# A two-product graph step with layer norm on one core: tiles in groups of four, sorted splits, two transpose banks

## The chip, the cores and the metric

The kernel runs on one core of a Trainium2 chip. Its time is the device time in microseconds, a median over runs. The matrix engine is called PE, its weight loads PEld, the vector engine DVE, the scalar engine ACT, GpSimd POOL, and SP is the engine that issues the transfers.

## What is computed

`adj` is 2048 x 2048 and `x` is 2048 x 512, both fp32:

```python
A_s  = (adj + adj.T) * 0.5 + eye(N)
deg  = sum(A_s, axis=1)
dinv = where(deg > 0, deg ** -0.5, 0)
y    = (adj @ (dinv[:, None] * A_s * dinv[None, :])) @ x
out  = layernorm(x + y, eps=1e-5)          # no scale, no shift
```

(In the reference `adj` is passed both as the matrix that is made symmetric and as the left factor.)

## The kernel before

The product is taken from the right. First u = dinv * (A_s @ (dinv * x)), which is the stage of the **steps**; then y = adj @ u, the stage of the **columns**. Both need fp32 precision from a reduced-precision product, so every operand is split into a high part (ACT rounds it) and a low part (DVE subtracts), and each product of a 128 x 128 tile with a 128 x 512 tile is three matmuls: high by high, high by low, low by high. There are 768 matmuls in the steps and 768 in the columns.

**A tile** is 128 rows of `adj`, there are 16. For each the kernel loads a strip (its rows, 128 x 2048) and needs the same columns turned. Tiles 0 to 3 are loaded as columns (`col`), turned by PE against the identity into a PSUM bank in four batches of four (`transpose_batch`), and copied to AT by ACT (`copy_turned`). Tiles 4 to 15 are loaded straight into AT (`load_pair`, two tiles in four transfers) in such a way that a 32 x 32 transpose on DVE (`turn`) finishes them. `sum_rows` adds the turned tile to the strip in place and sums the row, which is one DVE operation of 2048 elements; ACT takes the root of the degree, DVE inverts it, POOL refines it (DVE for tiles 0 to 3), and then `z_high` and `z_low` split dinv * x of the tile.

**A step** is one half (8 of the 16 row tiles) of one strip: `s_high` on ACT and `s_low` on DVE split 1024 columns of the strip into SH and SL, of which there are two pairs, and PE makes 24 matmuls over 8 banks (`step`). `SEGMENTS` lists the 32 steps: a segment keeps one half in the banks, and at its end the banks are saved (`save_part`, ACT) or added (`add_part`, DVE) to `part`. In the first segment only seven banks take part, since bank 7 is the one that the transposes of tiles 2 and 3 use; the eighth row tile's splits are kept in KH and KL and multiplied behind step 3 (`bank7_first_segment`). The second halves of tiles 8 to 11 are loaded and summed a second time (`load_again`, `sum_again`, `AGAIN`), because their strips are given away before.

**A pair of tiles** (4 and 5, 6 and 7, ...) interleaves its rows one by one: tile t has every second row. So the weights of a tile in a split half are every second column for tiles 4 to 15 and contiguous for 0 to 3 (`own_columns`, `half_weights`).

**The columns** are 32 halves of 24 matmuls, 16 column tiles by two halves (`HALVES`). `column_high` and `column_low` split 1024 elements of the turned matrix out of AT, one operation for the upper half and two of 512 for the lower. PE waits for `atl_done`. `layer_norm` follows each column tile.

**The order** on each engine is a list written out by hand in the code; every wait is on a semaphore of another engine. SP issues the transfers one after another and stands still at each of its waits: a strip waits until its place's last `s_low` is done, and an x tile for its buffer; the load of pair 8 waits for the end of step 3 and stands behind the strips and x tiles of tiles 4 to 7.

The lines in the profile that matter: L805 the transposes on PE, L817 to L861 the products of the steps, L897 to L899 the columns, L371 the copies of turned tiles, L389 and L391 `s_high`, L405 `z_high`, L432 `column_high`, L536 `turn`, L539 `sum_rows`, L588 `s_low`, L600 `z_low`, L620 `add_part`, L738 `column_low`.

## Time and profile before

| | us |
|---|---|
| median of 3 runs | 419.74 (418.32 to 422.92) |
| the profiled execution | 421.51 |
| its span, first to last instruction | 419.4 |
| PE busy in it | 381.2 (91%) |
| DVE busy | 244.6 (58%) |
| ACT busy | 118.4 (28%) |

The span is what the trace shows, and the profiled execution's time is 2.1 us more than it. The chain of waits is the work that ended last, followed back. Matmul starts are what to read of PE, since the ends are modelled and overlap the next matmul.

### The profile page before, as it was taken

The numbers are of one execution on the slowest core, as the hardware profiler recorded it, in microseconds if no ns is written. First come the engines' busy times: TensorE is split into PE (matmuls) and PEld (weight loads), VectorE is DVE, ScalarE is ACT, GpSimd is POOL, SyncE is SP. The second block draws the span as 40 slices with busy tenths as digits, with TensorE's granted clock in tenths as the row PEclk, the third lists the DMA queues.
The fourth block names the chain that finished last, engine by engine and source line by source line (L and its number), as shares of the span: only waits on it lengthen the run. The fifth ranks groups of instructions, "written<-read, shape, count | busy, mean of one in ns | idle before, by whom it ended". The sixth has DMA issues, their size and how long they took to land.

```text
span 419.4 us, 4227 instructions
## 1 busy us (share of the span) xinstructions
PE 381.2 (91%) x1600; PEld 308.8 (74%) x1600; DVE 244.6 (58%) x435; ACT 118.4 (28%) x186; POOL 23.6 (6%) x59
## 2 busy tenths in 40 slices
PE   3696699998999878998799999999999999999993
PEld 2575488776887756886588788888888888888882
DVE  1643638775739496679539952663444555555454
ACT  3443431315332112121326432222222112222210
POOL 0011101111031111002200000000000000000000
PEclk9998699999999988999899999999999999999999
DMA  7999139992799999430100000130111111111102
GB/s 233 337 346 186 52 107 245 315 184 72 213 218 279 272 243 308 152 100 25 52 26 0 2 0 2 50 101 2 50 50 52 50 50 52 50 51 51 34 31 86
DMA packets 68659, 49.54 MB, mean 118 GB/s; under 512 B 50848, under 2 KB 59040, under 8 KB 66720
## 3 DMA queue, kind: packets, MB, share of 16 engines
q1 hardware_dynamic: 68640, 49.29, 46.5%
q8 instruction: 12, 0.20, 0.2%
q14 instruction: 7, 0.06, 0.0%
HBM read 45.09 MB, written 4.19 MB: 118 GB/s over the span
## 4 chain that ended last, share of the span: by engine, by line
PE 64%; DVE 17%; DMA 6%; ACT 5%; issue 4%; SPq 3%; POOL 0%; ACTq 0%; DVEq 0%
PE bank L897 14%; PE bank L899 14%; PE bank L898 14%; PE bank L846 7%; PE bank L849 7%; PE bank L843 6%; DVE strip L539 5%; DVE SL L588 3%; DVE AT L536 3%; DMA col<-in_adj 2%; ACT SH L391 2%; DMA AT<-in_adj 2%; SPq L250 2%; DMA xr<-in_x 2%; PE bank L805 2%
## 5 line engine op out<-in xcount | busy, mean ns | idle before, releaser
L897 PE MATMUL bank<-UH,ATH 128*128 128x512 f32 x256 | 100.8, 394 | 0.4 <-DVE ATL L738 0.4
L899 PE MATMUL bank<-UH,ATL 128*128 128x512 f32 x256 | 100.7, 393 | 0.0
L898 PE MATMUL bank<-UL,ATH 128*128 128x512 f32 x256 | 100.5, 393 | 0.0
L738 DVE TENSOR_TENSOR ATL<-AT,ATH 128x512 fp32r<-128x512 f32 (+1 forms) x48 | 40.3, 867 | 77.2 <-ACT ATH L432 77.2
L432 ACT ACTIVATE ATH<-AT 128x512 fp32r<-128x512 f32 (+1 forms) x48 | 35.4, 768 | 84.1 <-PE bank L899 84.1
L897 PEld LDWEIGHTS bank<-UH,ATH 128*128 128x128 f32 x256 | 49.1, 192 | 11.0 <-DVE ATL L738 0.8
L588 DVE TENSOR_TENSOR SL<-strip,SH 128x1024 fp32r<-128x1024 f32 (+1 forms) x32 | 38.5, 1203 | 31.6 <-ACT SH L391 31.2
L849 PE MATMUL bank<-ZHr,SL 128*128 128x512 f32 x128 | 52.8, 413 | 4.4 <-DVE SL L588 4.4
L899 PEld LDWEIGHTS bank<-UH,ATL 128*128 128x128 f32 x256 | 49.1, 192 | 10.4
L898 PEld LDWEIGHTS bank<-UL,ATH 128*128 128x128 f32 x256 | 49.1, 192 | 10.2
L843 PE MATMUL bank<-ZHs,SH 128*128 128x512 f32 x117 | 48.2, 412 | 7.7 <-ACT ZHs L405 7.5
L846 PE MATMUL bank<-ZLr,SH 128*128 128x512 f32 x128 | 52.4, 410 | 2.8 <-DVE ZLr L600 2.8
L843 PE MATMUL bank<-ZHr,SH 128*128 128x512 f32 x128 | 52.4, 409 | 2.7 <-ACT SH L391 2.7
L539 DVE SCALAR_TENSOR_TENSOR strip<-strip,AT 128x2048 f32<-128x2048 f32 (+1 forms) x19 | 37.0, 1950 | 23.9 <-ACT AT L371 17.9
L846 PE MATMUL bank<-ZLs,SH 128*128 128x512 f32 x117 | 47.8, 409 | 3.3 <-DVE ZLs L600 3.3
L849 PE MATMUL bank<-ZHs,SL 128*128 128x512 f32 x117 | 47.1, 403 | 0.2 <-DVE SL L588 0.2
L391 ACT ACTIVATE SH<-strip 128x1024 fp32r<-128x1024 f32 x28 | 29.3, 1050 | 33.6 <-PE bank L849 33.5
L849 PEld LDWEIGHTS bank<-ZHr,SL 128*128 128x128 f32 x128 | 25.6, 200 | 11.4 <-DVE SL L588 6.1
L843 PEld LDWEIGHTS bank<-ZHs,SH 128*128 128x128 f32 x117 | 23.2, 198 | 13.3 <-ACT SH L389 8.1
L843 PEld LDWEIGHTS bank<-ZHr,SH 128*128 128x128 f32 x128 | 25.8, 202 | 9.3 <-ACT SH L391 4.0
L846 PEld LDWEIGHTS bank<-ZLr,SH 128*128 128x128 f32 x128 | 25.6, 200 | 9.0 <-DVE ZLr L600 3.5
L536 DVE STREAM_TRANSPOSE AT<-AT 128x2048 f32<-128x2048 f32 x12 | 27.6, 2303 | 5.6 <-DMA AT<-in_adj 5.6
(66 smaller groups left out, 281.4 us busy)
## 6 DMA issues: line engine op xcount, KB each, us to landing
strip<-in_adj SPq DMA_DIRECT2D x15, 1024.0 KB, 8.1
AT<-in_adj SPq DMA_DIRECT2D x24, 512.0 KB, 9.2
xr<-in_x SPq DMA_DIRECT2D x32, 256.0 KB, 2.9
out<-outr SPq DMA_DIRECT2D x16, 256.0 KB, 2.0
col<-in_adj SPq DMA_DIRECT2D x3, 1024.0 KB, 10.0
strip<-in_adj SPq DMA_DIRECT2D x4, 512.0 KB, 9.3
col<-in_adj SPq DMA_DIRECT2D x4, 256.0 KB, 5.0
strip<-in_adj SPq DMA_DIRECT2D x4, 256.0 KB, 5.3
```

The costliest lines, as they stand in the source:

```text
L391: nc.scalar.activation(SH[s % 2][:, :], s_half(s), ACT.Copy).then_inc(sh_done, 1)
L432: ins = nc.scalar.activation(half_place(ATH[i % 2], lo, hi, groups), src, ACT.Copy)
L536: nc.vector.transpose(v, v).then_inc(turned, 1)
L539: return nc.vector.scalar_tensor_tensor(out=strip[t % 4][:, cols], in0=strip[t % 4][:, cols], scalar=1.0, in1=turned_rows(t, cols.start, c ...
L588: nc.vector.tensor_tensor(SL[s % 2][:, lo:HALF], s_half(s)[:, lo:HALF], SH[s % 2][:, lo:HALF].bitcast(F32), ALU.subtract).then_inc(sl_done, 1)
L738: ins = nc.vector.tensor_tensor(half_place(ATL[i % 2], lo, hi, groups), src, half_place(ATH[i % 2], lo, hi, groups).bitcast(F32), ALU.subt ...
L843: nc.tensor.matmul(banks[b][:, :], wh, zh[:, :], start=first, stop=False)
L846: nc.tensor.matmul(banks[b][:, :], wh, zl[:, :], start=False, stop=False)
L849: nc.tensor.matmul(banks[b][:, :], wl, zh[:, :], start=False, stop=stop).then_inc(prod_done, 1)
L897: nc.tensor.matmul(bank[:, :], wh, UH[:, k, :], start=opens and n == 0, stop=False)
L898: nc.tensor.matmul(bank[:, :], wh, UL[:, k, :], start=False, stop=False)
L899: last = nc.tensor.matmul(bank[:, :], wl, UH[:, k, :], start=False, stop=ends)
```

## The change

- Tiles 4 to 15 come in **groups of four** (`GROUPS`): a tile has eight consecutive rows in every 32 (`R = 8`), instead of every second row. `load_block` loads four tiles by 2 parts of 1024 rows, in runs of 128 columns (512 bytes) instead of 64 (256 bytes); `turn` does half a tile (1024 elements) for each part, so there are 24 of them and not 12.
- The splits **sort** the columns (`sorted_pieces`): high and low are written so that each tile's 128 columns lie together. A step on half 0 takes two operations of 512 for it, one on half 1 one of 1024. The weights of all tiles are contiguous (`weights`, `half_weights`). In the columns both halves are split in two operations of 512.
- The **first segment** has four pairs SH and SL (`S_SLOT`), so that the splits of steps 0 to 3 all stay; steps 0 to 2 run on six banks (`early_step`), banks 6 and 7 take the transposes of tiles 1 to 3 in turn, and their share of steps 0 to 2 follows (`late_banks`) ahead of step 3. KH and KL are gone.
- The **second load** of the halves of tiles 8 to 11 is gone with its sums; `SEGMENTS` has another order of tiles, and the strips other places (`STRIP_SLOT`).
- x is loaded into the place of the low split (`XZ`), in seven places; an x tile waits for the products that used the place before, so on SP, where strips stand behind it.
- The **order lists** of ACT and DVE are new.

The core of the diff:

```diff
 Q = 32
+R = 8
...
-    PAIRS = range(NATURAL, NB, 2)
-    SEGMENTS = [(0, [0, 1, 2, 3]), (1, [0, 1, 2, 3, 4, 5, 6, 7]), (0, [4, 5, 6, 7, 8, 9, 10, 11, 12, 13]),
-                (1, [12, 13, 8, 9, 10, 11, 14, 15]), (0, [14, 15])]
+    EARLY = 3
+    LATE_BANKS = (6, 7)
+    GROUPS = range(NATURAL, NB, 4)
+    SEGMENTS = [(0, [0, 1, 2, 3]), (1, [0, 1, 2, 3, 4, 5, 6, 7]), (0, [4, 5, 6, 7, 8, 9, 10, 11]),
+                (1, [9, 10, 11, 8, 12, 13, 14, 15]), (0, [13, 14, 15, 12])]
     STEPS = [(t, half) for half, tiles in SEGMENTS for t in tiles]
     SEG_START = [sum(len(tiles) for _, tiles in SEGMENTS[:i]) for i in range(len(SEGMENTS) + 1)]
     S_END = len(STEPS)
...
+    STRIP_SLOT = [2, 3, 0, 1] * 3 + [3, 0, 1, 2]
+    S_SLOT = [s % 4 if s < HB else s % 2 for s in range(S_END)]
...
+            rows = ap[group_of(t) * P:(group_of(t) + 4) * P, :]
+            return rows.rearrange("(x k i) c -> k x i c", k=4, i=R)[t % 4]
...
+        def sorted_pieces(s, buf):
+
+            v = s_half(s)
+            if STEPS[s][1] == 0:
+                lo, hi = slice(0, HALF // 2), slice(HALF // 2, HALF)
+                return [(v[:, lo], buf[:, lo]),
+                        (v[:, hi].rearrange("p (x k i) -> p x k i", k=4, i=R),
+                         buf[:, hi].rearrange("p (k x i) -> p x k i", k=4, i=R))]
+            return [(v.rearrange("p (x k i) -> p x k i", k=4, i=R), buf.rearrange("p (k x i) -> p x k i", k=4, i=R))]
+
+        def weights(buf, half, b):
+
+            n = b if half == 0 else b % 4 * 2 + b // 4
+            return buf[:, n * P:(n + 1) * P]
...
+            def load_block(first, part):
+                rows = slice(part * HALF, (part + 1) * HALF)
+                for q in range(4):
+                    c0 = first * P + P * q
+                    dst = AT[Q * q:Q * (q + 1), first * N:(first + 4) * N].rearrange(
+                        "p (b e) -> p b e", e=P)[:, part * HALF // Q:(part + 1) * HALF // Q, :]
+                    src = adj[rows, c0:c0 + P].rearrange("(b r) c -> r b c", r=Q)
+                    sp.dma_start(dst, src).then_inc(block_in[first, part], 16)
 
...
+                t, slot = Z_TILES[k], z_slot(k)
+                if z_before(k) is not None:
+                    sp.wait_ge(prod_done, step_end(z_before(k)))
+                sp.dma_start(XZ[slot][:, :], own_rows(x, t)).then_inc(xz_in[slot], 16)
...
-            load_pair(4)
+            load_block(4, 0)
+            load_block(4, 1)
             load_strip(4)
             load_x(4)
             load_strip(5)
             load_x(5)
-            load_pair(6)
             load_strip(6)
             load_x(6)
             load_strip(7)
             load_x(7)
...
-            sp.wait_ge(prod_done, step_end(SEG_START[1]))
-            sp.wait_ge(zl_done, EARLY_X)
-            load_pair(8)
+            sp.wait_ge(tr_copied, CHUNKS * NATURAL)
+            load_block(8, 0)
+            load_block(8, 1)
+            load_x(8)
             load_strip(8)
-            load_x(8)
+            load_x(9)
             load_strip(9)
-            load_x(9)
-            load_pair(10)
+            load_x(10)
...
+            sp.wait_ge(prod_done, step_end(Z_LAST[7]))
+            load_block(12, 0)
             load_x(11)
+            load_block(12, 1)
+            load_x(12)
...
+                if s_before(s) is not None:
+                    act.wait_ge(prod_done, step_end(s_before(s)))
+                act.wait_ge(sum_done, t + 1)
+                if half == t // HB:
+                    act.wait_ge(diag_done, t + 1)
+                for src, dst in sorted_pieces(s, SH[S_SLOT[s]]):
+                    ins = nc.scalar.activation(dst, src, ACT.Copy)
...
+            def turn(t, part):
+
+                dve.wait_ge(block_in[group_of(t), part], 64)
+                v = turned_rows(t, part * HALF, (part + 1) * HALF)
+                nc.vector.transpose(v, v).then_inc(turned[t], 1)
...
+            def early_step(s, kinds, group=range(6)):
+
+                slot, zs = S_SLOT[s], z_slot(Z_OF_STEP[s])
+                for kind in kinds:
+                    if kind == "high":
+                        pe.wait_ge(sh_done, s + 1)
+                        pe.wait_ge(zh_done, s + 1)
+                    elif kind == "z low":
+                        pe.wait_ge(zl_done, s + 1)
+                    else:
+                        pe.wait_ge(sl_done, s + 1)
+                    w = SL[slot] if kind == "s low" else SH[slot]
+                    z = ZL[zs] if kind == "z low" else ZH[zs]
...
+                        ins = nc.tensor.matmul(banks[b][:, :], w[:, b * P:(b + 1) * P], z[:, :],
+                                               start=s == 0 and kind == "high", stop=False)
+                        if kind == "s low":
+                            ins.then_inc(prod_done, 1)
+
+            def late_banks(s):
+
+                slot, zs = S_SLOT[s], z_slot(Z_OF_STEP[s])
+                for b in LATE_BANKS:
+                    wh, wl = SH[slot][:, b * P:(b + 1) * P], SL[slot][:, b * P:(b + 1) * P]
+                    nc.tensor.matmul(banks[b][:, :], wh, ZH[zs][:, :], start=s == 0, stop=False)
+                    nc.tensor.matmul(banks[b][:, :], wh, ZL[zs][:, :], start=False, stop=False)
+                    nc.tensor.matmul(banks[b][:, :], wl, ZH[zs][:, :], start=False, stop=False).then_inc(prod_done, 1)
...
+            pe.wait_ge(tr_copied, CHUNKS)
+            transpose_batch(1, 0)
+            transpose_batch(1, 1)
+            early_step(0, ["high"])
+            transpose_batch(1, 2)
+            transpose_batch(1, 3)
+            early_step(0, ["z low", "s low"])
+            for t in range(2, NATURAL):
                 for n in range(CHUNKS):
                     transpose_batch(t, n)
-            first_step()
...
+                early_step(t - 1, ["high", "z low", "s low"])
+            pe.wait_ge(tr_copied, CHUNKS * NATURAL)
+            for s in range(EARLY):
+                late_banks(s)
+            for s in range(EARLY, S_END):
                 step(s)
```

The rows that follow are as the program issues them, engine by engine. PE at its start, before (bank and col are PSUM bank and column tile, the numbers are buffers):

```order
L805 MATMUL bank<-ident,col_70 128x128 x16
L805 MATMUL bank<-ident,col_71 128x128 x16
L817 MATMUL bank<-ZHs_74,SH_82 128x512 x4
L821 MATMUL bank<-ZLs_78,SH_82 128x512 x4
L825 MATMUL bank<-ZHs_74,SL_84 128x512 x4
L817 MATMUL bank<-ZHs_74,SH_82 128x512 x3
L821 MATMUL bank<-ZLs_78,SH_82 128x512 x3
L825 MATMUL bank<-ZHs_74,SL_84 128x512 x3
L805 MATMUL bank<-ident,col_72 128x128 x4
L843 MATMUL bank<-ZHs_75,SH_83 128x512
L846 MATMUL bank<-ZLs_79,SH_83 128x512
L849 MATMUL bank<-ZHs_75,SL_85 128x512
```

and with the change:

```order
L861 MATMUL bank<-ident,col_58 128x128 x16
L861 MATMUL bank<-ident,col_59 128x128 x8
L879 MATMUL bank<-ZH_74,SH_62 128x512 x6
L861 MATMUL bank<-ident,col_59 128x128 x8
L879 MATMUL bank<-ZL_81,SH_62 128x512 x6
L879 MATMUL bank<-ZH_74,SL_66 128x512 x6
L861 MATMUL bank<-ident,col_60 128x128 x16
L879 MATMUL bank<-ZH_75,SH_63 128x512 x6
L879 MATMUL bank<-ZL_82,SH_63 128x512 x6
L879 MATMUL bank<-ZH_75,SL_67 128x512 x6
L861 MATMUL bank<-ident,col_61 128x128 x16
L879 MATMUL bank<-ZH_76,SH_64 128x512 x6
```

Tile 2's four batches stood one by one between the products of step 1; now all four stand ahead of them, and the products come six at a time by kind.

DVE from the low split of step 19 on, with the change (AT is the turned matrix, part_52 the half sums, SL the low split, strip_54 to strip_57 the four strips):

```order
L616 TENSOR_TENSOR SL_67<-strip_55,SH_63 128x512
L616 TENSOR_TENSOR SL_67<-strip_55,SH_63 128x16x4x8
L557 STREAM_TRANSPOSE AT<-AT 128x128x8 x2
L622 SCALAR_TENSOR_TENSOR ZL_85<-XZ_92,dinv,ZH_78 128x512
L557 STREAM_TRANSPOSE AT<-AT 128x128x8
L634 TENSOR_TENSOR part_52<-bank,part_52 128x512
L616 TENSOR_TENSOR SL_66<-strip_57,SH_62 128x32x4x8
L634 TENSOR_TENSOR part_52<-bank,part_52 128x512
L557 STREAM_TRANSPOSE AT<-AT 128x128x8
L634 TENSOR_TENSOR part_52<-bank,part_52 128x512 x3
L616 TENSOR_TENSOR SL_67<-strip_54,SH_63 128x32x4x8
L634 TENSOR_TENSOR part_52<-bank,part_52 128x512 x2
```

Before, the adds of that segment stood together behind the low split of step 22, and a second sum of tile 8 followed:

```order
L588 TENSOR_TENSOR SL_84<-strip_54,SH_82 128x1024
L620 TENSOR_TENSOR part_52<-bank,part_52 128x512 x8
L588 TENSOR_TENSOR SL_85<-strip_55,SH_83 128x1024
L607 TENSOR_TENSOR strip_54<-strip_54,AT 128x1024
L610 TENSOR_TENSOR strip_54<-strip_54,twice 128x128
L600 SCALAR_TENSOR_TENSOR ZLr_92<-xr,dinv,ZHr_90 128x512
```

Turns of the next group and adds are now mixed with the splits. SP after the transfers of tile 3, before and with the change:

```order
L267 DMA xs_69<-in_x 128x512
L250 DMA AT<-in_adj 32x64x64 x4
L259 DMA strip_54<-in_adj 128x2048
L271 DMA xr<-in_x 128x512
L259 DMA strip_55<-in_adj 128x2048
L271 DMA xr<-in_x 128x512
L250 DMA AT<-in_adj 32x64x64 x4
L259 DMA strip_56<-in_adj 128x2048
```

```order
L282 DMA XZ_91<-in_x 128x512
L265 DMA AT<-in_adj 32x32x128 x8
L276 DMA strip_56<-in_adj 128x1x2048
L282 DMA XZ_88<-in_x 128x1x512
L276 DMA strip_57<-in_adj 128x1x2048
L282 DMA XZ_89<-in_x 128x1x512
L276 DMA strip_54<-in_adj 128x1x2048
```

Both parts of a group of four follow at once, where the second pair stood behind two strips.

## Rows read from the trace of the kernel before

**Rows 1.** The page: busy time by engine, and the chain's shares

```profile
PE 381.2 (91%) x1600; PEld 308.8 (74%) x1600; DVE 244.6 (58%) x435; ACT 118.4 (28%) x186; POOL 23.6 (6%) x59
...
PE 64%; DVE 17%; DMA 6%; ACT 5%; issue 4%; SPq 3%; POOL 0%; ACTq 0%; DVEq 0%
```

**Rows 2.** Busy time by stretch: PE, PEld, DVE, ACT, POOL, PEclk, DMA, GB/s

```profile
0.00:57.46 57.46, 38.49 (x160) 30.19 (x161) 24.02 (x56) 24.29 (x42) 4.52 (x11) 0.91 0.85 224
57.46:234.04 176.58, 164.20 (x673) 131.63 (x672) 125.73 (x159) 52.13 (x75) 19.05 (x48) 0.97 0.70 162
234.04:412.97 178.93, 178.54 (x769) 147.00 (x767) 91.81 (x211) 41.80 (x69) 0.00 (x0) 1.00 0.13 43
412.97:419.36 6.39, 0.00 (x0) 0.00 (x0) 3.02 (x10) 0.20 (x1) 0.00 (x0) 0.84 0.11 41
```

**Rows 3.** PE in time: start, us, line and tiles, idle before and releaser

```profile
14.72 3.56 PE L805 MATMUL bank<-ident,col 128*128 128x128 f32 x16 [3.84 <-DMA col<-in_adj]
...
34.78 0.49 PE L843 MATMUL bank<-ZHs,SH 128*128 128x512 f32 x1 [3.52 <-ACT ZHs L405]
...
47.21 0.77 PE L843 MATMUL bank<-ZHs,SH 128*128 128x512 f32 x1 [3.96 <-ACT ZHs L405]
...
57.46 0.39 PE L843 MATMUL bank<-ZHs,SH 128*128 128x512 f32 x1
```

**Rows 4.** ACT in time, tile 2: last copy, root, high split

```profile
29.45 0.60 ACT L371 ACTIVATE AT<-bank 128x512 f32<-128x512 f32 x1 [1.26 <-PE bank L805]
32.67 0.20 ACT L376 ACTIVATE root<-deg 128x1 f32<-128x1 f32 x1 [2.62 <-DVE deg L561]
32.95 0.95 ACT L389 ACTIVATE SH<-strip 128x896 fp32r<-128x896 f32 x1
```

**Rows 5.** Busy time by stretch, columns as in rows 2

```profile
25.00:30.00 5.00, 5.00 (x30) 4.22 (x29) 0.00 (x0) 1.74 (x3) 0.00 (x0) 1.00 1.12 357
30.00:33.00 3.00, 1.26 (x8) 0.86 (x6) 2.81 (x6) 0.30 (x3) 0.00 (x0) 1.00 1.30 218
36.00:39.00 3.00, 3.00 (x11) 2.43 (x12) 0.00 (x0) 0.60 (x1) 0.00 (x0) 0.58 1.36 207
```

**Rows 6.** PE in time: the first matmul after a stall

```profile
149.93 0.50 PE L849 MATMUL bank<-ZHr,SL 128*128 128x512 f32 x1 [2.44 <-DVE SL L588]
...
164.64 0.68 PE L846 MATMUL bank<-ZLr,SH 128*128 128x512 f32 x1 [1.42 <-DVE ZLr L600]
...
204.76 0.50 PE L846 MATMUL bank<-ZLr,SH 128*128 128x512 f32 x1 [1.42 <-DVE ZLr L600]
```

**Rows 7.** SP in time: when pair 8 is issued

```profile
109.64 10.22 SPq L250 DMA_DIRECT2D AT<-in_adj  x4
```

**Rows 8.** Transfers of line L259 (strips), issue to landing

```profile
DMA to landing us min/median/max: 5.1/8.1/12.1
```

**Rows 9.** Groups by shape: busy us, mean ns, idle before

```profile
L539 DVE SCALAR_TENSOR_TENSOR strip<-strip,AT 128x2048 f32<-128x2048 f32 x15 | 34.3, 2285 | 14.4 <-ACT AT L371 14.3
L588 DVE TENSOR_TENSOR SL<-strip,SH 128x1024 fp32r<-128x1024 f32 x28 | 34.1, 1220 | 31.4 <-ACT SH L391 31.2
...
L536 DVE STREAM_TRANSPOSE AT<-AT 128x2048 f32<-128x2048 f32 x12 | 27.6, 2303 | 5.6 <-DMA AT<-in_adj 5.6
...
L738 DVE TENSOR_TENSOR ATL<-AT,ATH 128x512 fp32r<-128x512 f32 x32 | 20.7, 688 | 29.2 <-ACT ATH L432 29.2
...
L432 ACT ACTIVATE ATH<-AT 128x512 fp32r<-128x512 f32 x32 | 18.4, 624 | 33.0 <-PE bank L899 33.0
```

**Rows 10.** PE in time, one half of the columns: every third matmul

```profile
344.57 0.39 PE L897 MATMUL bank<-UH,ATH 128*128 128x512 f32 x1
...
345.27 0.39 PE L897 MATMUL bank<-UH,ATH 128*128 128x512 f32 x1
...
347.34 0.39 PE L897 MATMUL bank<-UH,ATH 128*128 128x512 f32 x1
...
348.02 0.39 PE L897 MATMUL bank<-UH,ATH 128*128 128x512 f32 x1
```

625 lines of the change are left out of this document (299 added, 326 removed).

## The prediction

> **What bounds the kernel now.** First the busy time and the chain [rows 1]: PE is busy for 381 of 419 us and holds 64% of the chain, DVE 17%. So PE's work is the floor, and what can be won is where PE waits. The stretches [rows 2] say where. The columns, from 234.04 to 412.97, are 768 matmuls in 178.93 us, with PE busy for 178.54: nothing but PE counts there. The tail behind them is 6.39 us. The other 57 + 177 us hold the 32 steps. Step 4 starts at 57.46 [rows 3], and 28 steps of 24 matmuls fill 176.58 us.
>
> What such a step needs is read from every third matmul [rows 10]: a row tile takes 0.70 us (345.27 - 344.57) where its weights are every second column, and 0.68 us (348.02 - 347.34) where they are contiguous (tiles 0 to 3). I use 0.6825, the mean of three such neighbours, against 0.70. Of the 28 x 8 = 224 row tiles of steps 4 to 31, 16 x 8 + 12 x 4 = 176 are strided: 176 x 0.70 + 48 x 0.6825 = 156.0 us. So 176.6 - 156.0 = 20.6 us of that stretch are stalls, with what the clock lost behind them. They are short waits for a split or a z tile [rows 6]: 2.44, 1.42 and 1.42 us are the three longest; PE's clock falls to its lower level (1.2 of 2.4 GHz) after some of them, which the mean of 0.97 shows [rows 2].
>
> In the first stretch PE is busy for 38.5 of 57.5 us, and the clock has a mean of 0.91. Here the chain goes round once per tile: last copy of tile 2 at 29.45 + 0.60, sum on DVE, root on ACT at 32.67, high split at 32.95 [rows 4], first product of step 2 at 34.78 [rows 3]: 4.7 us. Tile 3 is 12.43 us later (47.21 - 34.78), so 7.7 us of each round pass from the first product to the last copy of the next tile, since its four batches wait for one bank and stand between products.
>
> **The change, part by part.** (1) *Start.* Tile 1's transposes still start at 14.72 [rows 3], behind its transfer. But six high products of step 0 now stand between its second and third batch. 16 transposes took 3.56 us, 0.89 per batch, at the low clock: two batches reach 16.5; the six products cost some 0.43 us each (twice the full-clock interval) until about 18 and 0.23 then, so 18.6; two more batches and the copies end at about 20.5. From there a round is: the 4.7 us chain, plus 0.3 us because the split of 896 is now two of 512 (2 x 0.624 against 0.95 [rows 4, 9]), plus four copies of 0.6 with one trip between the two banks, 2.6 us: 7.6 instead of 12.4. The last copies of tile 3 end at 20.5 + 2 x 7.6 = 35.7, and the inputs of step 3 are there at 40.7. PE is later than that: from the last batch of tile 2 at 27.1 it has 36 products of steps 1 and 2, 18 of the late banks, four batches of 0.44 (half of 0.89, at the full clock), a wait of 0.5, and I charge one low-clock piece of 3.4 us (1.7 us lost), as the 0.58 of 36 to 39 us before [rows 5] followed the 3.52 us of idling [rows 3]; here PE idles about 3.2 us ahead of tile 2's third batch. 54 x 0.2275 + 1.8 + 0.5 + 1.7 = 16.3, so 43.4. Step 3 is 5.5 us: **step 4 starts at 48.9 instead of 57.5**.
>
> (2) *Weights.* All row tiles are contiguous: 28 x 8 x 0.6825 = 152.9 us for the steps and 32 x 8 x 0.6825 = 174.7 for the columns. Against before that is 3.1 and 192 x 0.0175 = 3.4 us, 6.5 in all. The page "SBUF — State Buffer" of the Trainium skill (section on the DMA port swizzle) says that fp32 can be strided by up to 4 elements for free; by that rule the every-second-column weights cost nothing before, this gain is none, and the time is 6.5 us above mine. The 0.0175 us per row tile in [rows 10] speaks against it, and the measurement decides.
>
> (3) *Work of DVE in steps 4 to 31.* By [rows 9], per start-to-start (about 0.08 less than a duration): 24 half turns x 1.16 = 27.8, 12 sums x 2.46 (with their small operations) = 29.5, splits 16 x 1.16 + 12 x 1.24 = 33.4, 14 low z and 16 adds x 0.61 to 0.67 (as a 512-wide one), diagonals and roots 5: 115 us of 153. Before, its busy time was 126 of 177 with the overlaps [rows 2], some 118 counted in this way. The second sums (four of 1024 elements with a diagonal, 5.8 us) go, two-piece splits and halved turns give back 3. So DVE's work stays; what goes away must go by order and by transfers.
>
> (4) *Transfers.* The turned tiles came in 256-byte runs at 218 and 207 GB/s; the stretch with columns in 512-byte runs and strips moved 357 [rows 5]. Group 4 (4.2 MB) is issued behind tile 3 as a whole and lands by about 45 us. Group 8 waits only for the copies and for x of tile 7, so it is issued near 71 us instead of 109.64 [rows 7], long ahead of its use at step 16 (48.9 + 12 x 5.46 = 114.4). I find no turn that waits for it. The price is on SP: from tile 4 on a strip stands behind an x tile that waits for the end of a step. A lone strip lands after 5.1 us [rows 8]. For step 24: step 22 ends, 0.8 us of issue, 5.2 landing, sum 2.4, low z 0.7, root 0.1, split 1.2: 10.4 us after that end for the split that step 25 needs 10.9 + 0.5 us after it. Steps 24, 25 and 26 have **1.0 us of slack** each; with a contended landing of 8 us they would each wait 2.
>
> (5) *Ends of segments.* DVE adds bank 7 behind a turn: by its list, a walk with these durations has the add done 0.55 us after PE wants bank 7 of step 20: 0.7 with the refill. The other segment ends and the first columns have their inputs 2 us early or more, by the same walk. (6) *Columns.* Upper halves are split in two pieces, 2 x 0.624 + 2 x 0.688 = 2.6 us on ACT and DVE in a row, against 5.46 us of PE per half: covered. Without that cover it would cost 0.3 us a half.
>
> **The sum.** 48.9 + 152.9 + 174.7 + 0.3 (pipeline fill) + 6.4 (tail) = 383.2. Stalls: 0.7 at bank 7, 0.5 for the thin slack, 1.7 for one more low-clock piece, 2.9: a span of 386.1. The profiled execution was 2.1 above its span: 388.2, against 421.5. The median of before was 1.8 below that execution, which gives 386.4; I put the median at **387**. Unknown costs: stalls from 0 (384) to some 8 us (393).
>
> **Rivals.** *Weights gain nothing:* the 6.5 us are of the bank or the place, not of the stride: 387 + 6.5 = 394. For it only that the effect is tiny; against it that both kinds alternate within one bank. *The stalls stay:* DVE's work is as before and at 75% in a shorter stretch, and strips behind x tiles land at 8.1 us, the median [rows 8], not 5.1. Then steps lose their 20.6 us as now: 387 + 17.7 = 405. *The start stays cold:* idle pieces keep PE at 1.2 GHz from 22 to 43 us; 54 products at 0.43 instead of 0.2275 are 10.8 us, 1.7 already charged: 396. *Slower:* runs of eight elements cost DVE and ACT. Nothing in [rows 9] has such runs; a stride of two is free there (2285 ns for 2048 elements). The reordered forms are 90.7 us of DVE's 115. With 38 us of cover, DVE as the bound eats the 33 us gained when these forms take 1.8 times as long (115 + 0.8 x 90.7 = 187, against 153); at double they make the steps 206 us and the time 387 + 53 = 440.
>
> **How the numbers follow.** Forecast 0.64 (its own range 383 to 392), weights 0.12, cold start 0.07, stalls stay 0.12, slower strides 0.05. From 382 to 402 lie the first three and the lower part of the fourth, some 0.85. Within 1%, which is about what a measurement of this kernel can tell from no change, is 415.5 to 424: 0.03, from the two worst cases half met; slower 0.04; faster 0.93.
>
> **What would show it.** Step 4's first product near 49; one or two low-clock pieces, not four or five; row tiles of 0.68 us everywhere, the columns in 175 us; half turns at 1.2 us and sums at 2.3; PE's stalls from step 4 on below 5 us, the one of step 20 on an add, those of 24 to 26 on a split, if any; strips landing in 5 to 6 us. The prediction is wrong if DVE's new forms are slower than 1.3 us, or if the x waits on SP push strips behind their sums.

## The result

The changed kernel takes **393.83 us** (median of 4 runs, 389.11 to 397.95) against 421.33 (4 runs, 418.32 to 423.51), and the ratio is 0.929, 95% interval 0.919 to 0.940. Ratios, here and below, count only runs that are not over 1.5% above the fastest of their kernel, which leaves out 397.95 and 396.42 here (a fifth run, of 393.88, counts) and 397.12 in the repetition, so that they come out a little lower than the quotients of the medians. Repeated in five rounds it was 393.53 against 421.02, 0.933 (0.927 to 0.938). The forecast was 387 in 382 to 402, so sign and range held; the size was 7 us too good by the median, and just under 5 by the ratio (0.929 of 421.33 is 391.6). The profiled execution is the longest of its four, 397.95 us with a span of 395.3, so its parts hold some 4 us more than the median has. They are compared with the forecast's span of 386.1.

| us | before | forecast | after |
|---|---|---|---|
| step 4 starts | 57.46 | 48.9 | 50.26 |
| steps 4 to 31 | 176.58 | 155.8 | 164.33 |
| columns | 178.93 | 175.0 | 174.31 |
| tail | 6.39 | 6.4 | 6.40 |
| span | 419.4 | 386.1 | 395.3 |

The busy time of each engine and the shares of the chain that ended last (they answer to [rows 1]), after:

```profile
PE 368.1 (93%) x1600; PEld 300.0 (76%) x1600; DVE 240.7 (61%) x469; ACT 118.9 (30%) x212; POOL 31.9 (8%) x59
...
PE 74%; DMA 13%; DVE 6%; SPq 4%; ACT 1%; issue 1%; DVEq 0%; ACTq 0%
```

DVE's 17% of the chain has become 6%, and the transfers' 6% has become 13%, with 4% of SP's issuing beside it. That is the kernel's new weak place. The first three stretches, columns as in [rows 2]:

```profile
0.00:50.30 50.30, 36.47 (x161) 29.61 (x162) 29.33 (x61) 25.53 (x44) 1.76 (x11) 0.97 1.08 265
50.30:214.59 164.29, 157.40 (x674) 126.42 (x672) 115.68 (x174) 49.42 (x83) 30.09 (x48) 0.99 0.78 153
214.59:388.90 174.31, 174.24 (x769) 143.96 (x767) 92.68 (x227) 43.71 (x85) 0.00 (x0) 1.00 0.15 47
```

PE idles for 7 us in the steps, where it idled for 12, its mean clock there is 0.99 instead of 0.97, and DVE is busy for 116 us of 164. PE in time at the start, as in [rows 3]:

```profile
15.60 1.94 PE L861 MATMUL bank<-ident,col 128*128 128x128 f32 x8 [3.92 <-DMA col<-in_adj]
...
27.59 1.53 PE L861 MATMUL bank<-ident,col 128*128 128x128 f32 x8 [2.32 <-ACT AT L379]
28.78 2.90 PE L879 MATMUL bank<-ZH,SH 128*128 128x512 f32 x6
...
44.82 0.39 PE L906 MATMUL bank<-ZH,SH 128*128 128x512 f32 x1
...
45.50 0.39 PE L906 MATMUL bank<-ZH,SH 128*128 128x512 f32 x1
...
50.26 0.39 PE L906 MATMUL bank<-ZH,SH 128*128 128x512 f32 x1
```

The idle gaps of 3.52 and 3.96 us ahead of the first products of steps 2 and 3 have become one of 2.32 and one of 0.34, now ahead of transposes; the six products at 28.78 took 2.90 us, which is the lower clock, and between the cold start and step 4 that is the only such piece. A row tile's three matmuls take 0.68 us (45.50 - 44.82). PE's stalls in the steps answer to [rows 6]. These are six of nine, the five longest and the one at the last add. By counting 24 products a step they fall into steps 12, 19, 20, 23, 24 and 26 (the first step is 0):

```profile
95.18 0.50 PE L912 MATMUL bank<-ZH,SL 128*128 128x512 f32 x1 [0.79 <-DVE SL L616]
...
136.71 0.47 PE L906 MATMUL bank<-ZH,SH 128*128 128x512 f32 x1 [1.58 <-ACT ZH L401]
...
149.81 0.50 PE L906 MATMUL bank<-ZH,SH 128*128 128x512 f32 x1 [0.58 <-DVE part L634]
...
163.47 0.50 PE L912 MATMUL bank<-ZH,SL 128*128 128x512 f32 x1 [1.33 <-DVE SL L616]
...
169.96 0.50 PE L912 MATMUL bank<-ZH,SL 128*128 128x512 f32 x1 [0.70 <-DVE SL L616]
...
182.23 0.50 PE L912 MATMUL bank<-ZH,SL 128*128 128x512 f32 x1 [0.70 <-DVE SL L616]
```

The releaser named is DVE or ACT. What those two waited for in turn is a transfer, as DVE's own rows show:

```profile
56.66 3.50 DVE L557 STREAM_TRANSPOSE AT<-AT 128x1024 f32<-128x1024 f32 x3 [3.68 <-DMA AT<-in_adj]
...
89.33 4.62 DVE L557 STREAM_TRANSPOSE AT<-AT 128x1024 f32<-128x1024 f32 x4 [2.73 <-DMA AT<-in_adj]
...
100.53 3.50 DVE L557 STREAM_TRANSPOSE AT<-AT 128x1024 f32<-128x1024 f32 x3 [4.07 <-DMA AT<-in_adj]
...
134.26 2.37 DVE L557 STREAM_TRANSPOSE AT<-AT 128x1024 f32<-128x1024 f32 x2 [3.10 <-DMA AT<-in_adj]
...
159.74 2.29 DVE L560 SCALAR_TENSOR_TENSOR strip<-strip,AT 128x2048 f32<-128x2048 f32 x1 [3.91 <-DMA strip<-in_adj]
```

And ACT's row of the z that PE waits for at 136.71:

```profile
135.84 0.72 ACT L401 ACTIVATE ZH<-XZ,dinv 128x512 fp32r<-128x512 f32 x1 [6.01 <-DMA XZ<-in_x]
```

The half turns at 89.33 come 2.73 us late, the low split behind them too, and PE stalls at 95.18. At 136.71 PE waits for ACT's high part of z, whose x tile SP had issued only at 125.00, behind turned tiles; DVE's low part of it stood behind the half turns of 134.26. The sum at 159.74 is that of tile 12, first used in step 24; it waits for its strip, and the low split of step 23 is the next large operation behind it in DVE's list. So PE's stall at 163.47 is in step 23, and those of steps 24 and 26 follow in the same way from the sums of tiles 13 and 15. The groups by shape, as in [rows 9]:

```profile
L560 DVE SCALAR_TENSOR_TENSOR strip<-strip,AT 128x2048 f32<-128x2048 f32 x15 | 34.4, 2291 | 23.4 <-DMA strip<-in_adj 14.8 <-ACT AT L379 8.6
L557 DVE STREAM_TRANSPOSE AT<-AT 128x1024 f32<-128x1024 f32 x24 | 28.4, 1220 | 13.6 <-DMA AT<-in_adj 13.6
L616 DVE TENSOR_TENSOR SL<-strip,SH 128x1024 fp32r<-128x1024 f32 x16 | 19.4, 1210 | 2.2 <-ACT SH L394 2.0
...
L394 ACT ACTIVATE SH<-strip 128x1024 fp32r<-128x1024 f32 x16 | 16.9, 1053 | 15.6 <-PE bank L912 13.5 <-DVE strip L594 1.3 <-PE bank L891 0.8
```

Runs of eight elements cost DVE nothing: 2291 ns against 2285 for a sum, 1210 against 1220 for a split, and ACT's high split of 1024 takes 1053 ns. The idle time ahead of them is what is new. Last, the landing of strips (line L276), as in [rows 8]:

```profile
DMA to landing us min/median/max: 8.3/10.8/15.0
```

Before it was 5.1/8.1/12.1. The three strips that SP issues from 156 to 185 us, when no turned tile is in the queue (number, size, median us to landing), are no faster than 8 us:

```profile
strip<-in_adj SPq DMA_DIRECT2D x3, 1024.0 KB, 8.6
```

And SP, where the second group of four is issued, as in [rows 7]:

```profile
72.80 18.80 SPq L265 DMA_DIRECT2D AT<-in_adj  x8
```

It is issued 37 us earlier, as forecast, but SP needs 18.8 us to hand over these eight transfers, 2.35 us for each. Most x tiles and strips from 55 us on are handed over in 0.54 to 0.60 us in the same trace. I read the difference as a full queue; the trace shows the time, not the queue.

### The profile page after: what moved, and what is told of

It is laid out like the page before. It is cut to its first block, busy times and chain, and to the rows that moved or that the text cites. A ratio compares the mean times of both kernels' runs of the same rounds, so it can differ in the third digit from the quotient of the medians.

```text
span 395.3 us, 4276 instructions
## 1 busy us (share of the span) xinstructions
PE 368.1 (93%) x1600; PEld 300.0 (76%) x1600; DVE 240.7 (61%) x469; ACT 118.9 (30%) x212; POOL 31.9 (8%) x59
## 4 chain that ended last, share of the span: by engine, by line
PE 74%; DMA 13%; DVE 6%; SPq 4%; ACT 1%; issue 1%; DVEq 0%; ACTq 0%
PE bank L954 15%; PE bank L953 15%; PE bank L955 15%; PE bank L912 8%; PE bank L909 8%; PE bank L906 8%; DMA AT<-in_adj 6%; DMA strip<-in_adj 4%; PE bank L879 3%; SPq L265 3%; DMA col<-in_adj 3%; DVE AT L557 2%; DVE strip L560 2%; PE bank L861 2%; DVE SL L616 1%
## 5 line engine op out<-in xcount | busy, mean ns | idle before, releaser
L912 PE MATMUL bank<-ZH,SL 128*128 128x512 f32 x232 | 91.8, 396 | 4.5 <-DVE SL L616 4.5
L906 PE MATMUL bank<-ZH,SH 128*128 128x512 f32 x232 | 91.2, 393 | 2.2 <-ACT ZH L401 1.6
L909 PE MATMUL bank<-ZL,SH 128*128 128x512 f32 x232 | 91.3, 394 | 0.2 <-DVE ZL L622 0.2
L794 DVE TENSOR_TENSOR ATL<-AT,ATH 128x512 fp32r<-128x512 f32 x64 | 41.4, 688 | 72.1 <-ACT ATH L429 72.1
L429 ACT ACTIVATE ATH<-AT 128x512 fp32r<-128x512 f32 x64 | 36.9, 623 | 84.5 <-PE bank L955 80.7
L912 PEld LDWEIGHTS bank<-ZH,SL 128*128 128x128 f32 x232 | 44.0, 190 | 16.6 <-DVE SL L616 7.7
L906 PEld LDWEIGHTS bank<-ZH,SH 128*128 128x128 f32 x232 | 44.0, 189 | 12.1 <-issue 2.0
L909 PEld LDWEIGHTS bank<-ZL,SH 128*128 128x128 f32 x232 | 43.9, 189 | 10.1 <-DVE ZL L622 1.0
L394 ACT ACTIVATE SH<-strip 128x512 fp32r<-128x512 f32 (+1 forms) x48 | 35.2, 766 | 41.0 <-PE bank L912 38.4
L616 DVE TENSOR_TENSOR SL<-strip,SH 128x512 fp32r<-128x512 f32 (+1 forms) x48 | 39.9, 859 | 9.4 <-ACT SH L394 9.0
L557 DVE STREAM_TRANSPOSE AT<-AT 128x1024 f32<-128x1024 f32 x24 | 28.4, 1220 | 13.6 <-DMA AT<-in_adj 13.6
L861 PE MATMUL bank<-ident,col 128*128 128x128 f32 x64 | 12.8, 357 | 13.8 <-DMA col<-in_adj 11.2
L360 POOL TENSOR_SCALAR corr<-inv,deg 128x1 f32<-128x1 f32 x12 | 14.3, 1189 | 108.4 <-DVE inv L598 108.4
## 6 DMA issues: line engine op xcount, KB each, us to landing
strip<-in_adj SPq DMA_DIRECT2D x15, 1024.0 KB, 10.8
```

What stands on the lines that cost most here:

```text
L394: ins = nc.scalar.activation(dst, src, ACT.Copy)
L429: ins = nc.scalar.activation(half_place(ATH[i % 2], n, natural), src, ACT.Copy)
L557: nc.vector.transpose(v, v).then_inc(turned[t], 1)
L616: ins = nc.vector.tensor_tensor(low, src, high.bitcast(F32), ALU.subtract)
L794: ins = nc.vector.tensor_tensor(half_place(ATL[i % 2], n, natural), src, half_place(ATH[i % 2], n, natural).bitcast(F32), ALU.subtract)
L906: nc.tensor.matmul(banks[b][:, :], wh, ZH[zs][:, :], start=first, stop=False)
```

## The experiments

The theories that the runs had to tell apart: **the loads of turned tiles run at some 200 GB/s, not at 357**, and the steps' stalls come from that, against **the stalls are of order** (what stands in front of what on SP and DVE), with a third question, whether each saving is the size that was forecast. Medians are given with the 95% interval of the ratio to before, whose medians in the four sets were 421.02, 421.81, 420.44 and 420.11.

### The changed kernel again

> The changed kernel as it is, once more, as the measure for the runs beside it: 0.92 to 0.94 of before, 389 to 396 us. If its steps 4 to 31 hold the same stalls as in the first profile (11 to 12 us, on the low splits of steps 12, 17, 18, 24, 25 and 27, on z of step 19 and on the last add of step 20), they belong to the order and the transfers and not to one disturbed execution.

393.53 us (391.03 to 397.12), ratio 0.933 (0.927 to 0.938). In its profile nearly the same places stall: steps 12, 19 (on ACT's z, for 2.99 us), 20, 23, 24 and 26. (The expectations number the last three 24, 25 and 27, one too high.) DVE waited 15.5 us for turned tiles. The versions below are compared with this median; its own runs are 6 us apart, so that 4 us between two versions are only just told from nothing and 3 are not, and the stalls of the traces have to carry the reading. Both profiles of the changed kernel are of its longest executions (397.95 and 397.12), and a shorter one was not profiled. The nearest is that of "Strips ahead of x" below, at 391.75 us: it has the stalls of steps 12, 14 and 16 to 18 and 15.1 us of waits for turned tiles, but in step 19 only 0.32 us and no piece at the lower clock. So the waits for transfers belong to the kernel; how much of step 19's loss a run of 391 us has is open.

### Runs of 256 bytes again

```diff
-                    c0 = first * P + P * q
-                    dst = AT[Q * q:Q * (q + 1), first * N:(first + 4) * N].rearrange(
-                        "p (b e) -> p b e", e=P)[:, part * HALF // Q:(part + 1) * HALF // Q, :]
-                    src = adj[rows, c0:c0 + P].rearrange("(b r) c -> r b c", r=Q)
+                    for w in range(2):
+                        c0 = first * P + P * q + 64 * w
+                        dst = AT[Q * q:Q * (q + 1), first * N:(first + 4) * N].rearrange(
+                            "p (b e) -> p b e", e=P)[:, part * HALF // Q:(part + 1) * HALF // Q, 64 * w:64 * w + 64]
+                        src = adj[rows, c0:c0 + 64].rearrange("(b r) c -> r b c", r=Q)
...
```

> The loads of the turned tiles in runs of 256 bytes again, as before the change, with twice as many transfers; all else as changed. Theory A (32 destination partitions set the rate, the run length does not): 200 to 215 GB/s as with 512 bytes, time within 1% of the changed kernel. Theory B (the 512-byte runs are worth something): these stretches fall clearly below 200 GB/s, every group lands later, 4 us or more are lost at steps 12 to 20.

401.66 us, ratio 0.953 (0.948 to 0.958): 8 us slower than the changed kernel, as the second theory had it. DVE's waits for turned tiles grow to 19.8 us. The stretch from 31 to 51 us, in which group 4 comes, columns as in [rows 2], first the changed kernel and then this version:

```profile
31.00:51.00 20.00, 19.66 (x94) 16.17 (x93) 17.17 (x31) 13.80 (x23) 0.38 (x2) 0.99 1.21 200
...
31.00:51.00 20.00, 19.66 (x94) 16.26 (x93) 17.28 (x31) 13.94 (x23) 0.38 (x2) 0.99 1.23 177
```

The transfers are also half as large here and twice as many. That isn't what slows them: "Turned tiles in alternating quarters" below has the same number and size with 512-byte runs, and 216 GB/s. But the run length alone isn't the whole either, since the kernel before moved 207 and 218 GB/s with 256-byte runs [rows 5]. Why the same runs are slower in the new layout is open.

### All partitions at once

```diff
-                    dst = AT[Q * q:Q * (q + 1), first * N:(first + 4) * N].rearrange(
-                        "p (b e) -> p b e", e=P)[:, part * HALF // Q:(part + 1) * HALF // Q, :]
-                    src = adj[rows, c0:c0 + P].rearrange("(b r) c -> r b c", r=Q)
+                    b0 = part * HALF // Q + q * 8
+                    dst = AT[:, first * N:(first + 4) * N].rearrange("p (b e) -> p b e", e=P)[:, b0:b0 + 8, :]
+                    src = adj[rows, c0:c0 + P].rearrange("(b r) c -> r b c", r=P)
```

> The loads of the turned tiles write all 128 partitions (8 runs of 512 bytes each) instead of 32 partitions (32 runs each); same bytes, same runs, same number of transfers. The data then stand in wrong places, so the sums are of other elements; the work is the same. Theory A, the destination's 32 partitions set the 205 GB/s: these stretches run at 320 GB/s or more, DVE's 13.6 us of waits for turned tiles fall below 3, the stalls of steps 12 to 19 (7 us with the low clock piece) go, 5 to 8 us less than the changed kernel. Theory B, the short runs or the pattern in adj set it: still 200 to 215 GB/s and no difference.

The turned tiles then hold other elements than the product needs, so this version is for its time only. 389.39 us, ratio 0.922 (0.916 to 0.929), 4 us faster. The same stretch:

```profile
31.00:51.00 20.00, 19.66 (x93) 16.15 (x93) 17.05 (x31) 13.55 (x23) 0.38 (x2) 0.98 1.06 262
```

Same bytes, same run length, same number of transfers: 262 GB/s instead of 200. For group 8, from 73 to 93 us, it is 261 instead of 201. SP hands that group over in 13.15 us instead of 18.80, so how long it stands follows the transfers' rate. A rate of 262 is between the two theories (320 or more, and no difference). No half turn waits at all, and PE has no stall before 143 us; the columns start at 207.38 instead of 214.59. So the number of partitions that a transfer writes counts (203 against 262), and within the new layout the run length does (177 against 203); the stalls of steps 12 to 19 are of the transfers' rate. The order in which a transfer reads the rows of `adj` changed with the partitions (`r=P` for `r=Q`), and was not tried by itself. The stalls of steps 23 and 24 stay (1.57 and 0.70 us), as the waits for strips do (20.9 us).

### Turned tiles in alternating quarters

```diff
-                for q in range(4):
+                for q, w in [(q, w) for pair in ((0, 2), (1, 3)) for w in range(2) for q in pair]:
+                    b0 = part * HALF // Q + w * 16
...
-                        "p (b e) -> p b e", e=P)[:, part * HALF // Q:(part + 1) * HALF // Q, :]
-                    src = adj[rows, c0:c0 + P].rearrange("(b r) c -> r b c", r=Q)
+                        "p (b e) -> p b e", e=P)[:, b0:b0 + 16, :]
+                    src = adj[b0 * Q:(b0 + 16) * Q, c0:c0 + P].rearrange("(b r) c -> r b c", r=Q)
```

> The changed kernel with the turned tiles loaded in 16 transfers of 256 KB per group of four and part instead of 4 of 512 KB (8 per part), the 32-partition quarters in the order 0, 2, 0, 2, 1, 3, 1, 3; data and run length as in the changed kernel. Theory (neighbouring transfers that write different halves of the partitions overlap, as writing all 128 did in wide): these stretches rise from 202 towards 261 GB/s, 2 to 4 us less. Rival (each transfer runs by itself, or overlap is no help): 200 to 207 GB/s, within 1%.

**389.01 us** (386.62 to 389.66), ratio 0.925 (0.920 to 0.929): the lowest median of all, though not to be told from the 389.39 before it. The stretch:

```profile
31.00:51.00 20.00, 19.66 (x95) 16.22 (x94) 17.74 (x31) 14.41 (x24) 0.38 (x2) 1.00 1.23 216
```

Waits for turned tiles fall from 13.6 us in four places to 4.1 in three, with 6 to 8% more rate. The overlap that the theory wanted, towards 261 GB/s, didn't come. The late stalls stay (1.33, 0.55 and 0.47 us in steps 23, 24 and 26). Smaller pieces and the order of the quarters were changed together, so which of the two helps stays open. Together with the next edit it was not run.

### Strips ahead of x

```diff
-            load_x(12)
             load_strip(12)
-            load_x(13)
+            load_x(12)
             load_strip(13)
-            load_x(14)
+            load_x(13)
...
```

> On SP the strips of tiles 12 to 15 are issued ahead of the x tile that waits for the end of a step, instead of behind it; nothing else. Theory (strips behind the x waits make the low splits of steps 24 to 27 late): strips of tiles 13 to 15 are issued some 5 us earlier, the four stalls between 163 and 183 us (1.5, 1.0, 0.2 and 1.0 us) are gone, 3.5 to 4.5 us less. Rival (DVE has too much work there, or the strips wait for their place anyway): the stalls stay within 1 us of what they are.

390.42 us, ratio 0.926 (0.920 to 0.933): 3 us less by the medians, which the scatter doesn't tell from nothing. In the trace all stalls of steps 23 to 26 are gone; DVE waits 5.0 us for strips of 1 MB instead of 14.8. Of the earlier ones that of step 19 is small (0.32 us) and that of step 20 on the add longer (1.46), and the rest stays. So the late stalls belong to SP's order and the strips' landing, as the forecast's item on slack had it.

### Group 8 earlier on SP

```diff
             load_strip(4)
-            load_x(4)
             load_strip(5)
-            load_x(5)
             load_strip(6)
-            load_x(6)
-            load_strip(7)
-            load_x(7)
+            load_x(4)
             sp.wait_ge(tr_copied, CHUNKS * NATURAL)
             load_block(8, 0)
+            load_x(5)
+            load_strip(7)
+            load_x(6)
+            load_x(7)
             load_block(8, 1)
```

> On top of strips_first, SP issues the first part of group 8 behind the strips of tiles 4 to 6 and x of tile 4, before the x tiles that wait for the ends of steps 5 to 7. Theory (turned tiles of group 8 come late because their load stands behind these waits on SP): DVE's waits for turned tiles at 89 and 100 us go, with the stalls at steps 12, 14, 16, 17 and 18 (some 3 us), 2 to 4 us less than strips_first, so 386 to 388 us. Rival (the transfers as such are too slow): the waits only move to another place, less than 1 us.

398.0 us, ratio 0.943 (0.937 to 0.948): 4 us slower than the changed kernel, 7.6 slower than the run before it, on which it is built. SP, from 55 us on:

```profile
55.83 18.18 SPq L265 DMA_DIRECT2D AT<-in_adj  x4
74.05 2.56 SPq L282 DMA_DIRECT2D XZ<-in_x  x1
```

And PE's stall that follows:

```profile
85.86 0.76 PE L906 MATMUL bank<-ZH,SH 128*128 128x512 f32 x1 [4.35 <-ACT ZH L401]
```

The stalls from step 12 to 19 are gone and the waits for turned tiles down to 4.0 us, and the x tiles are late in their place. Four transfers take SP 18 us to issue, and everything behind stands. Neither the theory (2 to 4 us less) nor its rival (less than 1 us of difference) is what came. The next two runs go on from here:

> On top of sp_order, DVE takes the low z of tile 11 ahead of the turns of group 12, which wait for their transfer, and the adds at the end of segment 2 ahead of all but two of them. Theory (step 19 waits 1.6 to 3.0 us for z because DVE stands at a turn, and the clock falls behind it; step 20 waits for the last add behind a turn, 0.6 to 1.5 us): both stalls and the low-clock piece go, 3 to 5 us less than the changed kernel's share there, in all 383 to 386 us. Rival (the turns then come late for the sums of tiles 12 to 15): new stalls at steps 22 to 25 of 1 us or more each.

Here DVE's list had z's low part and the adds ahead of the half turns of the last group. 398.37 us, ratio 0.945 (0.940 to 0.951), where 383 to 386 was expected. The stall of step 19 on z and that of step 20 on the add are gone, and two of 3 and 4 us for x at 74 and 88 us hide it.

> dve_strips with the first part of group 8 issued behind x of tile 5 and the strip of tile 7, so ahead of x of tiles 6 and 7 only (in sp_order it stood ahead of x of tile 5 too, which then landed too late for step 9). Theory (the queue is full from 31 to 100 us, and only what stands ahead of what decides): no stall at steps 8 to 11, none at 12 to 18, 384 to 387 us. Rival (with some 205 GB/s for the turned tiles any earlier place makes an x tile late): a stall of 2 us or more at step 10 or 11, 388 us or more.

With DVE's new list, and group 8's first part behind x of tile 5 and the strip of tile 7: 399.27 us, ratio 0.948 (0.941 to 0.954). The rival came true. PE has a single long stall, in step 10, and ACT's row says what it comes from:

```profile
91.57 0.79 PE L906 MATMUL bank<-ZH,SH 128*128 128x512 f32 x1 [8.88 <-ACT SH L394]
```

```profile
89.85 0.72 ACT L401 ACTIVATE ZH<-XZ,dinv 128x512 fp32r<-128x512 f32 x1 [14.38 <-DMA XZ<-in_x]
```

The x tiles of 6 and 7 were issued at 80.00, and behind the 8.88 us PE ran at the lower clock for 6.7 us (until 98.27). Neither earlier place for group 8 pays. The page's slices of transfer time of the changed kernel suggest why; a slice is 9.9 us, and the 16 DMA engines are busy for 90% or more in all from 10 to 138 us, so that whatever is put earlier puts something else later:

```profile
DMA  7999999999999965980001000310011111111102
```

> strips_first with the order on DVE of reordered (low z of tile 11 and the adds of segment 2 ahead of the turns of group 12), and SP's order around group 8 as in the changed kernel. Theory: the z stall of step 19, the last-add stall of step 20 and any low-clock piece behind them go; the small stalls at steps 12 to 18 stay, since group 8 is as late as before. 1 to 3 us less than strips_first, 386 to 389 us. Rival (the turns come too late for the sums of tiles 12 to 15): stalls of 1 us or more at steps 24 to 27, no gain.

DVE's new list, with SP's strips ahead of x and group 8 where it was: 391.6 us, ratio 0.932 (0.926 to 0.937), within the scatter of 390.4. In the trace the stall of step 20 is gone and that of step 19 is 0.16 and 0.23 us, with 0.3 us each in steps 24 to 26 in their place. The list alone is worth nothing that these runs can tell.

### One bank for the early transposes

```diff
-            return banks[n] if t == 0 else banks[LATE_BANKS[n % 2]]
+            return banks[n] if t == 0 else banks[7]
...
-                if t >= 1 and (t > 1 or n >= 2):
-                    pe.wait_ge(tr_copied, b - 1)
+                if t >= 1:
+                    pe.wait_ge(tr_copied, b)
```

> The changed kernel with one bank (7) for the transposes of tiles 1 to 3 instead of two in turn; bank 6 stays unused by them, all else as changed. Theory (the two banks shorten each round of the start): each tile's four copies take 4 to 5 us instead of 2.8, step 4 begins 2 to 5 us later. Rival (PE's 54 products set the start): less than 1 us.

398.57 us, ratio 0.944 (0.939 to 0.949): the second bank is worth 5 us. Two of ACT's four copies of tile 2, which now come 1.7 to 1.9 us apart:

```profile
30.02 0.60 ACT L379 ACTIVATE AT<-bank 128x512 f32<-128x512 f32 x1 [1.14 <-PE bank L861]
31.89 0.60 ACT L379 ACTIVATE AT<-bank 128x512 f32<-128x512 f32 x1 [1.27 <-PE bank L861]
```

Step 3 starts at 53.18 instead of 44.82, 8.4 us later, more than the 2 to 5 us expected. Part of it is clock and not order: the six high products of step 1 take 2.84 us (2.90 in the changed kernel), but those of step 2 take 2.79 where the changed kernel has 1.64; here PE had idled ahead of three single batches of tile 3. Of the 8.4 us 3 come back: the transfers have had more time, and the later stalls are fewer (3.4 us of idling instead of 6.9).

### The kernel before with contiguous weights

```diff
-  wh, wl = own_columns(SH[s % 2], m, half), own_columns(SL[s % 2], m, half)
+  wh, wl = (buf[:, m % HB * P:(m % HB + 1) * P] for buf in (SH[s % 2], SL[s % 2]))
```

and the same in `half_weights`.

> The kernel before, with every matmul of the steps from step 1 on and of the columns reading contiguous weights (the products are then of other columns; number and size of all operations as before). Theory (the stride of the weights costs 0.0175 us per row tile): all row tiles take 0.68 us, the columns 175.3 instead of 178.9 us, and 3.4 to 6.5 us less in all, since the part in the steps may go into stalls for DVE. Rival (something else of tiles 4 to 15 than the stride made them slow): row tiles stay at 0.70 us, no difference.

415.22 us against 421.81, ratio 0.985 (0.980 to 0.991), that is 6.2 us by the ratio (4.0 to 8.4). Steps and columns:

```profile
57.46:227.96 170.50, 157.82 (x673) 126.11 (x672) 125.14 (x158) 51.63 (x74) 19.02 (x48) 0.99 0.70 168
227.96:403.00 175.04, 174.18 (x768) 143.80 (x767) 92.01 (x211) 42.14 (x70) 0.00 (x0) 1.00 0.13 43
```

The columns lose 3.9 us, where the forecast's 192 row tiles make 3.4. The steps lose 6.1, more than the 3.1 of their weights; this profile is of the fastest of six runs, and its mean clock there is 0.99 instead of 0.97. By the rule of the Trainium skill's page "SBUF — State Buffer" (section on the DMA port swizzle), that four fp32 can be strided for free, the time would be 421.8 here. These runs speak against it for PE's weights.

### Single rows instead of runs of eight

```diff
-R = 8
+R = 1
```

> The changed kernel with one number changed: R is 1 and not 8, so of a group of four every tile has every fourth row (as a pair's tile had every second before), instead of eight rows in every 32. Groups, 512-byte runs, sorted splits and all orders stay, and the rows and columns stay consistent. In the changed kernel a strip of tiles 4 to 15 lands 8.3 us or more after its issue, where a lone one took 5.1 before. Theory (the eight-row pattern makes the strips and x tiles slow): the least time to landing is 5.1 to 5.6 us again, DVE's waits for strips (20.7 us) fall below 10, the stalls of steps 24 to 27 (4 us) go, 4 to 8 us less than the changed kernel, 386 to 389 us. Rival 1 (strips are slow since the queue is full of turned tiles): 8 us or more as now, time within 1%. Rival 2 (DVE and ACT pay for elements 16 bytes apart): sums above 2.4 us and half turns above 1.3 us, time equal or worse. The rate of the turned tiles stays at 200 to 215 GB/s by all.

**434.3 us** (433.06 to 435.93), ratio 1.034 (1.029 to 1.040): slower than the kernel before, where 386 to 389 was expected: the second rival came true. One row in four means that the sums, the half turns and the column splits go through AT in elements 16 bytes apart. The splits of the steps are another case: they read the strip in order and write, by `sorted_pieces`, every element 1 KB away from the last (512 bytes in the pieces of half 0). Groups by shape:

```profile
L560 DVE SCALAR_TENSOR_TENSOR strip<-strip,AT 128x2048 f32<-128x2048 f32 x15 | 52.9, 3526 | 5.1 <-ACT AT L379 5.1
...
L557 DVE STREAM_TRANSPOSE AT<-AT 128x1024 f32<-128x1024 f32 x24 | 47.5, 2041 | 0.0
...
L360 POOL TENSOR_SCALAR corr<-inv,deg 128x1 f32<-128x1 f32 x12 | 40.6, 3379 | 113.0 <-DVE inv L598 113.0
...
L394 ACT ACTIVATE SH<-strip 128x1024 fp32r<-128x1024 f32 x16 | 32.7, 2067 | 17.7 <-PE bank L912 15.7 <-DVE strip L594 2.1
L616 DVE TENSOR_TENSOR SL<-strip,SH 128x1024 fp32r<-128x1024 f32 x16 | 31.5, 1978 | 2.5 <-ACT SH L394 2.4
```

Sums, half turns and low splits take 1.54, 1.67 and 1.63 times as long as in the changed kernel, ACT's high splits 1.96 times, and the steps take 202.17 us instead of 164.33:

```profile
49.30:251.47 202.17, 172.44 (x674) 133.53 (x672) 170.54 (x176) 69.63 (x86) 60.88 (x48) 0.92 0.49 125
251.47:426.00 174.53, 174.36 (x768) 144.08 (x768) 110.32 (x228) 64.08 (x85) 0.00 (x0) 1.00 0.14 46
```

DVE is busy for 84% of the steps, and no sum and no half turn of tiles 4 to 15 waits for a transfer. In the columns the slower splits (971 ns instead of 688 for 512 elements on DVE) cost nothing, since PE's 5.46 us per half cover them. This is the forecast's fourth rival made real; the change escaped it by its runs of eight. One thing more came back: strips landed in 4.7/7.0/12.8 us, where the changed kernel's took 8.3/10.8/15.0. A slower kernel asks less of its transfers, so the fairest comparison is the last four strips, with no turned tile about: 6.2 to 7.6 us instead of 8.3 to 8.9. So the eight-row pattern costs a strip some 2 us there. The x tile ahead of each strip has the same pattern, and the two were not told apart.

## Why the forecast was right, and where it was off

**The start** was 1.4 us late, 50.26 for 48.9: PE got to tile 1's transposes 0.9 us later than the 14.72 that the forecast kept, and the rest is the round. The low-clock piece was one, as charged. One bank instead of two costs 8.4 us at step 3 in its experiment, and only 5 us of that reach the end, which fits a later part that is limited by transfers; the forecast added its terms as if they didn't touch.

**The weights** were right: 6.5 us forecast, 6.2 measured in the kernel before, and 0.68 us per row tile everywhere. The rival "weights gain nothing" (394) gives the right time by accident and is refuted.

**DVE's work** was close. Its operations were right, with sums and splits within 1% of the old ones and half turns at 1.22 us (the forecast's 1.16 from start to start). The 115 us forecast in the steps and the 116 measured agree by luck, though: the forecast's count stood at 118 before, where the busy time was 126. Like for like the busy time of the steps fell by 10 us (125.73 to 115.68), where the count fell by 3; 5 us of that moved ahead of step 4 (24.02 to 29.33), and 4 are gone. The rival of slower strides was rightly told apart from the change, but its price was too low: with factors of about 1.6 the forecast's formula gives 115 + 0.6 x 90.7 = 169 us of DVE, 16 above PE's 153, and so 387 + 16 = 403; the measured time is 434.3. A saturated engine is not needed for this: DVE is busy for 84% there, and PE idles for 30 us in the steps and runs at a mean clock of 0.92. POOL's small operations grow as well (below). The split of the 31 us that the formula lacks was not measured.

**The transfers** are the step that failed. "The stretch with columns in 512-byte runs and strips moved 357", which the forecast took over for the turned tiles because the runs are of 512 bytes. That stretch writes 128 partitions per transfer, and `load_block` writes 32. Measured is 200 to 203 GB/s, no more than the 218 and 207 of [rows 5] with 256-byte runs. Within the new layout the longer run was worth something, since with 256 bytes it has 177; and all partitions give 262, so that a part of the way to 357 stays unexplained. The page "SBUF — State Buffer" of the Trainium skill, in the section on the DMA port swizzle, says that bandwidth goes by how many of 16 ports the partitions reach, that 32 partitions reach eight of them, and that these carry at most some 218 GB/s. The trace agrees: from 31 to 51 us it is 177 to 216 in every version of the changed kernel whose transfers write 32 partitions, and 262 in the one whose transfers write 128. An estimate by that page's 218 GB/s makes group 4 (4.2 MB) 19 us of transfer. By the measured 203 it is 21, instead of the 12 that 357 GB/s make; its last half turns waited until 56.66, where "lands by about 45" was forecast. "I find no turn that waits for it", said of group 8, was wrong twice (2.73 and 4.07 us), and groups 4 and 12 were waited for as well (3.68 and 3.10): 13.6 us of DVE.

**The strips** were the second part of this step. "Strips landing in 5 to 6 us" rested on the minimum of [rows 8]. They took 8.3 us at least, and 8.6 with nothing turned in the queue, and so the forecast's own alternative came in: "with a contended landing of 8 us they would each wait 2". The forecast named steps 24, 25 and 26; the stalls were in 23, 24 and 26, with 1.33, 0.70 and 0.70 us. Step 23 was left out, whose low split stands behind the sum of tile 12. So the mechanism was right and the place nearly, and the chosen end of the bound was the wrong one. Strips ahead of x remove all three.

**The stalls** summed to 11.4 us (164.33 - 152.9), for which 2.9 were forecast: the nine waits with their refills are 8.5, a low-clock piece behind that of 136.71 is 1.7 (as charged), and 1.2 is spread. The add of bank 7 had 0.7 and was 0.58, at the step named. So 387 became 393.8: by the profiled spans, 1.4 at the start, 8.5 in the steps, and 0.7 less in the columns make the 9.2 between 386.1 and 395.3; the medians leave 7. "The stalls stay" (405) is half met, with 11.4 us instead of 20.6, in part by the strips' landing that it named (8.1 us) and in part by the turned tiles, which it didn't name. The measured 393.83 is above the forecast's own range of 383 to 392, and inside 382 to 402 only because that range also covers the rivals, and not by a right account of the transfers.

## What to carry to other kernels

Take the rate of a transfer only from a row with the same number of partitions at its destination; here 32 partitions instead of 128 cost 23% of the rate, and half the run length 13% within one layout, while another layout moved as much with the short runs. When a stall is taken from an engine by order, ask what its inputs' transfers will do in the shorter time, and weigh the engine that issues them: when the DMA engines are busy throughout, a big load holds everything behind it, so neither earlier place helped. Smaller pieces in another order did, by 4.5 us; strips ahead of less urgent tiles took their stalls away, for a gain within the scatter. When layouts are interleaved, keep runs: eight neighbours cost nothing, and single elements 16 bytes apart or scattered cost DVE 1.5 to 1.7 times and ACT up to twice.
